# Starting a recurrent layer's first group beside the last projections and norms of the attention layer before it

## The chip, the cores and the metric

The kernel runs on one core of one Trainium2 chip. The metric is the device time of one execution in microseconds (us), as the median of several runs. All matrix work is in float32.

## What is computed

Four layers follow one another on a hidden state of 16 sequences x 100 tokens x 512 channels: a grouped-query cross-attention (layer 0, 32 query heads, 8 key heads, 361 context tokens), a recurrent block of the RWKV kind (layer 1), a cross-attention with an MLP (layer 2), and a second recurrent block (layer 3). The two that the change touches, cut down:

```python
# layer 0, end: attention output, residual, norm
out = out @ Wo + bo
x = out + hidden_state
mu, var = x.mean(-1), x.var(-1)
x = (x - mu) * rsqrt(var + 1e-6) * gamma + beta

# layer 1, start (the "front")
xa = _ln(x, ln1_w, ln1_b)
sx = concatenate([state[:, 1:2] - xa[:, :1], xa[:, :-1] - xa[:, 1:]], axis=1)
xxx = tanh((xa + sx * maa_x) @ maa_w1).reshape(b, l, 5, DM)
xxx = einsum('blfd,fde->blfe', xxx, maa_w2)
xk, xw, xv, xr, xg = xa + sx * (maa_stack + xxx)      # five mixes
w = exp(-exp(time_decay + tanh(xw @ td_w1) @ td_w2))
r, k, v = xr @ Wr.T, xk @ Wk.T, xv @ Wv.T             # then a scan over the tokens
```

## The kernel before

The hidden state X stays in on-chip memory, channels on the partitions: 4 channel chunks (C = 4) of 128, and 1600 tokens along the free axis. There are 8 groups of 200 tokens (N = 200, two sequences each), and 4 pairs of groups. Each engine has its own instruction stream, in order; the streams meet only in semaphores. A signal's value at(i, n) counts n events of turn i, and an engine waits for it with wait_ge.

**The end of layer 0** works on pairs. For a pair t TensorE does two projections of one group each (project, line 314, 16 matmuls, which the trace counts as 32 records) into banks 4, 5 and 6, 7. DVE adds bias and residual in 8 instructions (line 1468). The norm of a pair (class Norm) takes, for each group: four accumulated matmuls for the mean (line 237), DVE's centring of 800 elements (line 243), ACT's square (247), four accumulated matmuls for the variance (252), on ACT a logarithm (258) and an exponential (261), each with a load of its table, DVE's scaling (266), and four affine activations on ACT into X (1547). The matmuls for pair t+1's projection stand behind the variances of pair t in TensorE's stream (behind_it), DVE's residual of pair t+1 behind its scaling of pair t. The loop has 3 turns, and a fourth norm without a projection stands behind it. All of layer 0 is over with the signal norm_ready.at(pairs), which layer 1 knows as after.done.

**The front of layer 1.** Function rwkv builds body(i, g, front, rec, back, tail) for every engine; a turn holds the front of group g+1, the recurrence of group g (rec), the output and the second norm of group g-1 (back) and the end of the MLP part of group g-2 (tail). turns() calls it first with the front of group 0 alone. Before that every engine waits for after.done, and for its weights. In the front: mean (bank 7), centring, square, variance, logarithm, exponential, scaling, affine into xs (963), the token shift on DVE (800, 804), the hidden projection on TensorE (600, 602), tanh on ACT (1010, 1011), and then five mixes, each four small matmuls (523), four DVE instructions (mix_term, 731) and an addition on POOL (1087), followed by projections (509). K's first half is evicted by ACT (1024), V's first half too (925). V goes through SP's queue to memory and comes back spread over the partitions (448, 465); with it, and with a start column from ACT (914), DVE can begin the recurrence: product (708) and scan (723). SP's stream waits for "columns", three small DVE memsets.

Layer 1's weights lie over buffers of layer 0 that are free once attention is over, so SP loads all of them from then on (L_w in the trace).

**Layer 2** already has the class FoldedNorm: DVE adds the four channel chunks in two instructions (lines 281 and 283 for the mean, 292 and 294 for the variance), and TensorE then needs one matmul where Norm has four (287, 298); its logarithms and exponentials are separate calls (302, 307), so two groups can share a table load. Its query loop (projection 314, evictions 1927) is in the trace of before as well.

Of the kernel before, what the change touches and what calls it, by code (L numbers as in the profile page):

```python
# [15 lines left out]
C = D // P  # L16
# [134 lines left out]
class Layer:  # L151
# [3 lines left out]

    def __init__(self, sync, tensor, vector, scalar, gpsimd, done, early, left, pieces):
        self.sync, self.tensor, self.vector, self.scalar, self.gpsimd = sync, tensor, vector, scalar, gpsimd
        self.done, self.early, self.left, self.pieces = done, early, left, pieces

# [232 lines left out]
def rwkv(core, m, name, base, after):  # L392
# [78 lines left out]
    occ = base // G  # L471

    def turns(eng, body):
# [12 lines left out]


    def tensor(pe):
        def body(i, g, front, rec, back, tail):
# [55 lines left out]
            if front:  # L545
                m.n1.pe_var(pe, f)
            if back:
                reduce(7, b)
# [46 lines left out]
            if front:  # L595
# [90 lines left out]
    def vector(dve):  # L686
        def body(i, g, front, rec, back, tail):
# [61 lines left out]
            if front:  # L749
# [3 lines left out]
                if back:  # L753
                    wait(dve, "bonus_sum", b, 1)
                m.n1.dve_center(dve, xg(g + 1), f)

            step(1)
# [18 lines left out]
            if front:  # L776
                m.n1.scale(dve, f)

            step(3)
# [15 lines left out]
            if front:  # L795
# [7 lines left out]
                for c in range(C):  # L803
                    dve.scalar_tensor_tensor(seq(m.xx)[:, c], seq(m.sx)[:, c], vec("maa_x", c), m.xs[:, c, :, 1:E],
                                             ALU.mult, ALU.add).then_inc(sem("xa_shifted"), 1)

            step(6)
# [21 lines left out]
            if front:  # L829
                if rec:  # L830
                    wait(dve, "k_sum", i, 2)
                mix_term(0)
            if back:
                wait(dve, "out_sum", b, 2)
# [8 lines left out]
            if front:  # L843
                if rec:
                    wait(dve, "decay", i, 4)
                mix_term(1)

            step(10)
# [12 lines left out]
            if front:  # L861
                if rec:
                    wait(dve, "r_sum", i, 2)
                mix_term(3)

# [25 lines left out]

        core.wait_before(dve, after)
        wait(dve, "weights", occ + 1)

        dve.memset(m.we.rearrange("p c j (b e) -> p (c j b) e", b=NB)[:, :, 0:1], 0.0).then_inc(sem("columns"), 1)
        dve.memset(m.k.rearrange("p c b e -> p (c b) e")[:, :, 0:1], 1.0).then_inc(sem("columns"), 1)
        dve.memset(m.v.rearrange("p c b e -> p (c b) e")[:, :, 0:1], 0.0).then_inc(sem("columns"), 1)
        turns(dve, body)


    def scalar(act):
        def body(i, g, front, rec, back, tail):
# [44 lines left out]
            if front:  # L947
                if tail:
                    act.wait_ge(m.n2.nrm.sem, m.n2.nrm.at(t, 1))
                m.n1.act_rstd(act, f)  # L950
            if back:
                if tail:
# [5 lines left out]
            if front:  # L958
# [3 lines left out]
                for c in range(C):  # L962
                    act.activation(m.xs[:, c, :, 1:E], seq(m.n1.yc)[:, c], ACT.Identity, bias=vec("ln1_b", c),
                                   scale=vec("ln1_w", c)).then_inc(sem("xa"), 1)
            if back:
                wait(act, "head_var", b, 1)
# [39 lines left out]
            if front:  # L1006
                wait(act, "mix_hidden_sum", f, 1)
                if rec:
                    wait(act, "mix_sum", i, 5)
                act.activation(m.tha, chunk(7, 0), ACT.Tanh).then_inc(sem("mix_hidden"), 1)  # L1010
                act.activation(m.thl[BACK:BACK + DM, :], chunk(7, 1, BACK, BACK + DM), ACT.Tanh).then_inc(
                    sem("mix_hidden"), 1)

            start(10)
# [102 lines left out]
def gqa_attention(core, name, after):  # L1117
# [101 lines left out]
    def tensor(pe):  # L1219
# [126 lines left out]

        def output(t):

            for u in range(2):
                pe.wait_ge(residual_added.sem, residual_added.at(t))  # L1350
                src = lambda k: qT[:, k, bass.ds(t * (2 * N) + u * N, N)]
                project(pe, core, 2 + u, Wo, src).then_inc(out_sum.sem, 1)

        def behind_it(t, more):

            for u in range(2):
                pe.wait_ge(residual_added.sem, residual_added.at(t, 4 * u + 4))
                norms[u].pe_mean(pe, lambda c: X[:, c, bass.ds(t * (2 * N) + u * N, N)], t)
            for u in range(2):
                norms[u].pe_var(pe, t)  # L1360
            if more:
                for u in range(2):
                    pe.wait_ge(residual_added.sem, residual_added.at(t, 4 * u + 4))
                    project(pe, core, 2 + u, Wo,
                            lambda k: qT[:, k, bass.ds(t * (2 * N) + 2 * N + u * N, N)]).then_inc(out_sum.sem, 1)

        output(0)
        with pe.Fori(0, pairs - 1) as t:
            behind_it(t, True)
        behind_it(pairs - 1, False)  # L1370


    def vector(dve):
# [84 lines left out]

        def xo(t, u):
            return X[:, :, bass.ds(t * (2 * N) + u * N, N)]  # L1460

        def residual(t):

            for u in range(2):
                dve.wait_ge(out_sum.sem, out_sum.at(t, u + 1))
                x = xo(t, u)
                for c in range(C):
                    dve.scalar_tensor_tensor(x[:, c, :], part(2 + u, c), vec_("bo", c), x[:, c, :], ALU.add,
                                             ALU.add).then_inc(residual_added.sem, 1)

        def behind_it(t, more):
            for u in range(2):
                dve.wait_ge(residual_added.sem, residual_added.at(t, 4 * u + 4))
                dve.wait_ge(norm_ready.sem, norm_ready.at(t))
                norms[u].dve_center(dve, xo(t, u), t)
            for u in range(2):
                norms[u].scale(dve, t)
            if more:
                residual(t + 1)

        residual(0)
        with dve.Fori(0, pairs - 1) as t:
            behind_it(t, True)
        behind_it(pairs - 1, False)


    def scalar(act):
# [50 lines left out]
        turns(act, step)  # L1538
        with act.Fori(0, pairs) as t:
            for u in range(2):  # L1540
                norms[u].act_square(act, t)
            for u in range(2):
                norms[u].act_rstd(act, t)
            for u in range(2):
                norms[u].wait_scaled(act, t)
                for c in range(C):
                    act.activation(X[:, c, bass.ds(t * (2 * N) + u * N, N)], norms[u].yc[:, c, :], ACT.Identity,
                                   bias=vec_("beta", c), scale=vec_("gamma", c)).then_inc(norm_ready.sem, 1)


    def gpsimd(pool):
# [31 lines left out]
        for u in range(2):  # L1583
# [3 lines left out]
                 (attention_ready.sem, attention_ready.at(TURNS)), left,  # L1587
                 (pairs, lambda t: (norm_ready.sem, norm_ready.at(t, 8))))

# [733 lines left out]
```

## Time and profile before

| | us |
|---|---|
| median of 3 runs (3078.34 to 3083.32) | 3081.06 |
| the profiled execution's own time | 3076.93 |
| its span in the profile | 3075.0 |
| TensorE busy (share of the span) | 2811.2 (91%) |
| DVE busy | 2003.5 (65%) |
| ACT busy | 1350.9 (44%) |
| POOL busy | 665.0 (22%) |
| mean granted TensorE clock (1 is 2.4 GHz) | 0.962 |

The profile is of one execution. All stretches further down are in us from the start of its span. A busy engine is not an engine at its peak: matmuls are pipelined, and their ends are modelled.

### The profile page before, as it was taken

Reading aid. Unit: us, or ns where it says so; the run is one execution under the profiler, and the core shown is the slowest. Engines: PE = TensorE matmul, PEld = TensorE weight load, DVE = VectorE, ACT = ScalarE, POOL = GpSimd, SP = SyncE. Lnnn points to the kernel's source line nnn. Section 1 sums busy time; section 2 is a strip of 40 time slices with the busy share of each in tenths; the row PEclk is TensorE's granted clock in tenths of the full one; section 3 lists DMA queues with packets and bytes.
Section 4 is the critical chain, followed back from the end, with each engine's and each line's share of the span. In section 5 each row is a group of like instructions: output and inputs, shape, how many; then the busy total and the mean of one; then the engine's idle time right before and its main releaser. Section 6 shows DMA issues by size and latency. Waiting matters only on the chain.

```text
span 3075.0 us, 53764 instructions
## 1 busy us (share of the span) xinstructions
PE 2811.2 (91%) x18112; PEld 2186.9 (71%) x18112; DVE 2003.5 (65%) x4888; ACT 1350.9 (44%) x3446; POOL 665.0 (22%) x436
## 2 busy tenths in 40 slices
PE   7999999967999999779999999999997889999986
PEld 7555555856888888666555455799996768888866
DVE  2878787338999999644555556511101699999993
ACT  1888888542443443343444444332311234444432
POOL 0111110015444444300000000000000454444440
PEclk9999999978999999889999999999998899999998
DMA  2100100313333333300000000300002333333340
GB/s 107 36 24 34 34 23 13 130 41 98 92 92 90 88 91 92 107 27 10 30 20 19 26 22 10 126 26 1 0 1 89 92 95 92 89 92 92 87 126 14
DMA packets 96167, 182.85 MB, mean 59 GB/s; under 512 B 10122, under 2 KB 87498, under 8 KB 92462
## 3 DMA queue, kind: packets, MB, share of 16 engines
q1 hardware_dynamic: 96046, 181.27, 19.2%
q8 instruction: 72, 1.18, 0.2%
q14 instruction: 49, 0.40, 0.0%
HBM read 171.34 MB, written 9.90 MB: 59 GB/s over the span
## 4 chain that ended last, share of the span: by engine, by line
PE 66%; DVE 12%; issue 9%; ACT 8%; DMA 2%; POOL 1%; SPq 0%; DVEq 0%; ACTq 0%; POOLq 0%
PE psum L509 19%; PE psum L314 10%; PE psum L1859 6%; PE psum L1746 4%; PE psum L1303 3%; DVE psum L708 3%; PE psum L500 3%; ACT arena L1506 3%; ACT arena L2126 2%; PE psum L1759 2%; PE psum L1801 2%; PE psum L516 2%; PE psum L1315 2%; DVE arena L723 2%; PE psum L523 2%
## 5 line engine op out<-in xcount | busy, mean ns | idle before, releaser
L509 PE MATMUL psum<-arena 128*128 128x200 f32 x4096 | 772.1, 347 | 51.5 <-DVE arena L876 18.6
L509 PEld LDWEIGHTS psum<-arena 128*128 128x128 f32 x4096 | 721.9, 198 | 135.6 <-issue 79.3
L1107 POOL TENSOR_TENSOR arena<-arena 128x800 f32<-128x800 f32 x256 | 454.9, 1780 | 452.2 <-DVE psum L708 452.2
L723 DVE TENSOR_TENSOR_SCAN arena<-arena,psum 128x808 f32<-128x808 f32 x256 | 470.0, 1836 | 37.3 <-PE psum L500 22.1
L314 PE MATMUL psum<-arena 128*128 128x200 f32 (+1 forms) x1920 | 332.1, 335 | 15.0 <-POOLq L139 13.3
L314 PEld LDWEIGHTS psum<-arena 128*128 128x128 f32 x1920 | 328.5, 192 | 16.7 <-POOLq L139 13.3
L1506 ACT ACTIVATE arena<-arena 100x361 f32<-100x361 f32 x512 | 300.6, 590 | 87.2 <-DVE arena L1417 85.5
L1087 POOL TENSOR_TENSOR arena<-arena 128x800 f32<-128x800 f32 x80 | 140.6, 1757 | 807.6 <-DVE arena L731 632.3
L708 DVE TENSOR_TENSOR psum<-arena 128x808 f32<-128x808 f32 x256 | 280.6, 1096 | 5.5
L1417 DVE CUSTOM_DVE_ANT_0 arena<-psum,arena 100x361 f32<-100x361 f32 x512 | 254.3, 531 | 45.4 <-ACT arena L1506 37.9
L1303 PEld LDWEIGHTS psum<-arena 100*128 100x128 f32 x1536 | 146.3, 142 | 131.2 <-ACT arena L1518 60.3
L2126 ACT ACTIVATE arena<-arena 100x361 f32<-100x361 f32 x256 | 149.6, 587 | 146.5 <-DVE arena L1999 146.5
L1303 PE MATMUL psum<-arena 100*128 100x100 f32 x1536 | 189.5, 258 | 24.3 <-ACT arena L1518 24.1
L1801 PEld LDWEIGHTS psum<-arena 100*128 100x128 f32 x768 | 84.5, 141 | 148.8 <-issue 74.8
L1759 PE MATMUL psum<-arena 128*128 128x512 f32 (+1 forms) x384 | 189.4, 605 | 0.0
L1746 PE MATMUL psum<-arena 128*128 128x361 f32 x512 | 180.2, 477 | 1.6 <-DVE arena L1927 1.5
L1859 PE MATMUL psum<-arena 128*128 128x200 f32 x1024 | 175.0, 333 | 0.1
L1859 PEld LDWEIGHTS psum<-arena 128*128 128x128 f32 x1024 | 173.4, 190 | 0.4 <-DMA arena<-L_fc 0.4
L914 ACT ACTIVATE arena<-arena 128x8 f32 (+1 forms) x256 | 54.1, 212 | 267.7 <-DMA arena<-v_rows 266.7
L247 ACT ACTIVATE arena<-arena 128x800 f32<-128x800 f32 x56 | 48.7, 870 | 262.3 <-DVE arena L243 262.1
L731 DVE SCALAR_TENSOR_TENSOR arena<-psum,arena 128x200 f32<-128x200 f32 x320 | 112.9, 415 | 57.8 <-PE psum L523 57.8
L500 PE MATMUL psum<-arena 128*32 128x400 f32 x1024 | 127.6, 537 | 23.8 <-POOL arena L1107 14.2
(142 smaller groups left out, 3908.3 us busy)
## 6 DMA issues: line engine op xcount, KB each, us to landing
arena<-v_rows SPq DMA_DIRECT2D x512, 202.0 KB, 3.2
arena<-ctxT SPq DMA_DIRECT2D x32, 722.0 KB, 4.2
arena<-L_w SPq DMA_DIRECT2D x9, 1024.0 KB, 10.5
arena<-L_w SPq DMA_DIRECT2D x8, 1152.0 KB, 16.1
v_rows<-arena SPq DMA_DIRECT2D x32, 202.0 KB, 2.1
arena<-L_fc SPq DMA_DIRECT2D x4, 1024.0 KB, 8.3
arena<-L_pj SPq DMA_DIRECT2D x4, 1024.0 KB, 15.5
arena<-xT SPq DMA_DIRECT2D x4, 800.0 KB, 12.0
```

The costliest lines, as they stand in the source:

```text
L314: mm = pe.matmul(core.part(w, m), weight[:, k, m * P:(m + 1) * P], src(k), start=k == 0, stop=k == k_chunks - 1)
L500: mm = pe.matmul(psum[r0:r0 + 32, 6, 0:2 * N], core.red_w[:, 24 - 8 * q:56 - 8 * q], rv[:, h, :, 0:L], start=q == 0, stop=q == 3)
L509: mm = pe.matmul(chunk(bank, j), m.W[n][:, k, c * P:(c + 1) * P], src[:, k, :], start=k == 0, stop=k == C - 1)
L708: dve.tensor_tensor(m.kv.rearrange("p (h x) -> p h x", h=2), kb, m.spread[n % 4].rearrange("p h a e -> p h (a e)"), ALU.mult).then_inc(sem ...
L723: dve.tensor_tensor_scan(m.ring[n % 4].rearrange("p j e -> p (j e)"), m.we[:, cc].rearrange("p j e -> p (j e)"), m.kv, 0.0, ALU.mult, ALU. ...
L1107: pool.tensor_tensor(sv, sv, rb, ALU.mult).then_inc(sem("r_states"), 1)
L1303: mm = pe.transpose(bank[4 + 3 * (n % 2)][:, j * L:(j + 1) * L], pr[h % 8][0:L, j * P:(j + 1) * P], ident[0:L, 0:L])
L1417: dve.tensor_tensor_reduce(out=sm[n][0:L], in0=bank[n][0:L, 0:S], in1=nmask[u][0:L], scale=1.0, scalar=FLT, op0=ALU.add, op1=ALU.min, accu ...
L1506: act.activation(pr[k % 8][0:L, 0:S], sm[n][0:L], ACT.Exp, bias=nmx[0:L, k:k + 1], scale=-1.0, accum_out=den[0:L, k:k + 1]).then_inc(exp_r ...
L1746: mm = pe.matmul(bank[6 + c % 2][:, 0:S], Wk[:, k, c * P:(c + 1) * P], ctxt[u % 2][:, k, :], start=k == 0, stop=k == C - 1)
L1759: mm = pe.matmul(bank[6 + j % 2][0:n, :], ctxt[u % 2][:, k, a:a + n], Wv[:, k, :], start=k == 0, stop=k == C - 1)
L1859: mm = pe.matmul(part(2 + q % 2, m), fc[:, k, j * P:(j + 1) * P], norms[u].yc[:, k, :], start=k == 0, stop=k == C - 1)
```

## The change

There are three parts.

- Layer 0's norms become FoldedNorm, with one table load for the logarithms and one for the exponentials of a pair.
- The loop at the end of layer 0 has two turns in place of three, in another order: TensorE does the first projection of pair t+1, the means of pair t, the second projection of pair t+1, the variances of pair t.
- What is left of layer 0 (the projections of pair 3, the norms of pairs 2 and 3) is handed to layer 1 as after.tail, three functions for TensorE, DVE and ACT. The first body() of rwkv, with the front of group 0 alone, calls them through rest() at fixed places. It starts when pair 0 is normalized (after.pieces[1](0)) instead of when layer 0 is over; the wait for after.done comes behind it, on DVE ahead of the fourth mix term, where the memsets of the columns now stand.

```diff
     def turns(eng, body):
-        core.wait_before(eng, after)
+        if after.tail:
+            eng.wait_ge(*after.pieces[1](0))
+        else:
+            core.wait_before(eng, after)
         wait(eng, "weights", occ + 1)
         body(base - 1, -1, front=True, rec=False, back=False, tail=False)
+        if after.tail:
+            core.wait_before(eng, after)
...
                 m.n1.pe_mean(pe, lambda c: X[:, c, ds(g + 1, N)], f)
+                rest(0, pe, "out 6", front, rec)
...
                 m.n1.pe_var(pe, f)
+                if not rec and after.tail:
+                    rest(0, pe, "means 2", front, rec)
+                    pe.wait_ge(m.n1.lnv.sem, m.n1.lnv.at(f, 1))
+                    rest(0, pe, "out 7", front, rec)
...
                 mm.then_inc(sem("mix_hidden_sum"), 1)
+                rest(0, pe, "means 3", front, rec)
...
                 mix(0)
+                rest(0, pe, "variances 3", front, rec)
...
                 wait(pe, "mixed", f, 2)
+                rest(0, pe, "bank 3 read", front, rec)
...
-    norms = [Norm(core, told, u, 1, 2 * u, 2 * u + 1).memory(r) for u in range(2)]
+    folds = s("folds", 8)
+    norms = [FoldedNorm(core, told, u, 1, 2 * u, 2 * u + 1).memory(r).signals(folds) for u in range(2)]
...
+        for u in range(2):
+            pe_output(pe, 0, u, True)
+        with pe.Fori(0, pairs - 2) as t:
+            pe_output(pe, t + 1, 0, False)
+            pe_means(pe, t)
+            pe_output(pe, t + 1, 1, False)
+            pe_variances(pe, t)
+        pe.wait_ge(residual_added.sem, residual_added.at(pairs - 2, 8))
...
+    p, z = pairs - 2, pairs - 1
+    def pe_tail(pe, k):
+        if k == "out 6":
+            pe_output(pe, z, 0, False)
+        if k == "means 2":
+            pe_means(pe, p)
+        if k == "out 7":
+            pe_output(pe, z, 1, False)
+            pe_variances(pe, p)
+            pe.wait_ge(residual_added.sem, residual_added.at(z, 8))
+        if k == "means 3":
+            pe_means(pe, z)
+        if k == "variances 3":
+            pe_variances(pe, z)
+        if k == "bank 3 read":
+            pe.wait_ge(norms[1].lnv.sem, norms[1].lnv.at(z, 2))
+    def dve_tail(dve, k):
+        if k == "centre 2":
+            dve_fold(dve, p)
+            dve_residual(dve, z, 0)
+            dve_centre(dve, p)
+        if k == "squares 2":
+            dve_squares(dve, p)
+        if k == "centre 3":
+            dve_residual(dve, z, 1)
+            dve_scale(dve, p)
+            dve_fold(dve, z)
+            dve_centre(dve, z)
+        if k == "squares 3":
+            dve_squares(dve, z)
+        if k == "scale 3":
+            dve_scale(dve, z)
+    def act_tail(act, k):
+        if k == "squares 2":
+            act_squares(act, p)
+        if k == "rstd 2":
+            act_rstd(act, p)
+        if k == "norm 3":
+            act_affine(act, p)
+            act_squares(act, z)
+            act_rstd(act, z)
+            act_affine(act, z)
+    def dve_centre(dve, t):
+        for u in range(2):
+            dve.wait_ge(norm_ready.sem, norm_ready.at(t))
+            norms[u].dve_center(dve, xo(t, u), t)
+        with dve.Fori(0, pairs - 2) as t:
+            dve_fold(dve, t)
+            dve_residual(dve, t + 1, 0)
+            dve_centre(dve, t)
+            dve_squares(dve, t)
+            dve_residual(dve, t + 1, 1)
+            dve_scale(dve, t)
+        with act.Fori(0, pairs - 2) as t:
+            act_squares(act, t)
+            act_rstd(act, t)
+            act_affine(act, t)
```

On DVE the pieces stand behind the front's centring (centre 2), its scaling (squares 2), the token shift (centre 3), mix term 0 (squares 3) and mix term 1 (scale 3); on ACT behind the front's exponential (squares 2), the affine into xs (rstd 2) and the tanh of the hidden projection (norm 3). The new dve_centre waits for norm_ready.at(t), that is, for all affines of the pairs before t, as behind_it did.

## Rows read from the trace of the kernel before

**Rows 1.** Busy time by stage: us, busy us of each engine, granted clock, DMA share, GB/s.
```profile
551.80:632.10 80.30, 68.42 (x384) 64.43 (x384) 26.76 (x48) 48.10 (x72) 0.00 (x0) 0.97 0.31 124
632.10:678.60 46.50, 33.86 (x144) 28.25 (x144) 11.72 (x32) 11.09 (x23) 6.93 (x4) 0.75 0.08 23
```
**Rows 2.** Chain that ended last, pieces in order of time: start, us, what.
```profile
582.41 1.63 PE psum L237 x8
584.18 1.00 DVE arena L243
585.20 0.88 ACT arena L247
586.12 1.62 PE psum L252 x8
587.74 10.84 PE psum L314 x64
...
600.28 1.63 PE psum L237 x8
```
**Rows 3.** Timeline, first projections of layer 0's end: start, us, engine, line, work, idle before.
```profile
551.85 11.10 PE L314 MATMUL psum<-arena 128*128 128x200 f32 x64 [0.70 <-DVE arena L1451]
...
562.98 1.43 DVE L1468 SCALAR_TENSOR_TENSOR arena<-psum,arena 128x200 f32<-128x200 f32 x4 [3.99 <-PE psum L314]
```
**Rows 4.** Timeline, one turn of layer 2's query loop, with folded norms.
```profile
1371.19 0.57 DVE L281 TENSOR_TENSOR arena<-arena 128x400 f32 x1
1371.79 0.37 DVE L283 TENSOR_TENSOR arena<-arena 128x200 f32<-128x200 f32 x1
...
1373.54 5.58 PE L314 MATMUL psum<-arena 128*128 128x200 f32 x32
...
1378.96 0.84 PE L298 MATMUL psum<-arena 128*128 128x200 f32 x4
...
1381.98 1.89 DVE L266 TENSOR_TENSOR arena<-arena 128x800 f32<-128x800 f32 x2 [1.26 <-ACT arena L307]
...
1383.79 0.57 DVE L281 TENSOR_TENSOR arena<-arena 128x400 f32 x1
```
**Rows 5.** Timeline, the norm of layer 0's last pair.
```profile
616.27 1.52 PE L237 MATMUL psum<-arena 128*128 128x200 f32 x8
...
621.73 1.28 ACT L258 ACT_TABLE_LOAD   x1
...
623.02 0.43 ACT L258 ACTIVATE arena<-psum,arena 128x200 f32<-128x200 f32 x1
...
628.46 3.65 ACT L1547 ACTIVATE arena<-arena 128x200 f32 x8
```
**Rows 6.** Busy time in one turn of layer 0's last loop.
```profile
581.00:599.00 18.00, 17.17 (x99) 16.25 (x98) 6.79 (x13) 12.03 (x18) 0.00 (x0) 1.00 0.00 0
```
**Rows 7.** Timeline, layer 1's front of group 0.
```profile
637.26 3.04 PE L252 MATMUL psum<-arena 128*128 128x200 f32 x8 [2.06 <-ACT arena L247]
...
648.01 3.03 PE L600 MATMUL psum<-arena 128*128 128x200 f32 x8 [7.71 <-DVE arena L804]
...
650.97 1.93 PE L602 MATMUL psum<-arena 128*32 128x200 f32 x8
...
658.72 4.59 PE L509 MATMUL psum<-arena 128*128 128x200 f32 x16 [0.28 <-POOL arena L1087]
...
671.20 0.50 ACT L925 ACTIVATE arena<-psum 128x400 f32<-128x400 f32 x1 [4.48 <-PE psum L509]
...
678.54 1.00 DVE L708 TENSOR_TENSOR psum<-arena 128x808 f32<-128x808 f32 x1
```
**Rows 8.** Busy time and granted clock (third last column) in slices of 1 us.
```profile
623.00:624.00 1.00, 0.38 (x3) 0.07 (x1) 0.00 (x0) 0.97 (x3) 0.00 (x0) 1.00 0.00 0
...
628.00:629.00 1.00, 0.00 (x0) 0.00 (x0) 0.41 (x1) 0.99 (x4) 0.00 (x0) 0.50 0.00 0
...
651.00:652.00 1.00, 1.00 (x5) 0.61 (x5) 0.00 (x0) 0.00 (x0) 0.00 (x0) 0.60 0.00 0
```

More of the change, by code:

```diff
@@ L471, in rwkv, with rest @@
     occ = base // G
+    def rest(n, eng, k, front, rec):
+        if front and not rec and after.tail:
+            after.tail[n](eng, k)
     def turns(eng, body):
-        core.wait_before(eng, after)
+        if after.tail:
+            eng.wait_ge(*after.pieces[1](0))
+        else:
+            core.wait_before(eng, after)
         wait(eng, "weights", occ + 1)
         body(base - 1, -1, front=True, rec=False, back=False, tail=False)
+        if after.tail:
+            core.wait_before(eng, after)
         wait(eng, "weights_back", occ + 1)
@@ L755, in body @@
                 m.n1.dve_center(dve, xg(g + 1), f)
+                rest(1, dve, "centre 2", front, rec)
             step(1)
@@ L777, in body @@
                 m.n1.scale(dve, f)
+                rest(1, dve, "squares 2", front, rec)
             step(3)
@@ L805, in body @@
                                              ALU.mult, ALU.add).then_inc(sem("xa_shifted"), 1)
+                rest(1, dve, "centre 3", front, rec)
             step(6)
@@ L832, in body @@
                 mix_term(0)
+                rest(1, dve, "squares 3", front, rec)
             if back:
@@ L846, in body @@
                 mix_term(1)
+                rest(1, dve, "scale 3", front, rec)
             step(10)
@@ L863, in body @@
                     wait(dve, "r_sum", i, 2)
+                if not rec and after.tail:
+                    dve.wait_ge(*after.done)
+                    columns()
                 mix_term(3)
@@ L890, in body, with columns @@
             step(15)
[L892 to L897, printed above, removed]
+        def columns():
+            dve.memset(m.we.rearrange("p c j (b e) -> p (c j b) e", b=NB)[:, :, 0:1], 0.0).then_inc(sem("columns"), 1)
+            dve.memset(m.k.rearrange("p c b e -> p (c b) e")[:, :, 0:1], 1.0).then_inc(sem("columns"), 1)
+            dve.memset(m.v.rearrange("p c b e -> p (c b) e")[:, :, 0:1], 0.0).then_inc(sem("columns"), 1)
+        if not after.tail:
+            core.wait_before(dve, after)
+            wait(dve, "weights", occ + 1)
+            columns()
         turns(dve, body)
@@ L950, in body @@
                 m.n1.act_rstd(act, f)
+                rest(2, act, "squares 2", front, rec)
             if back:
@@ L964, in body @@
                                    scale=vec("ln1_w", c)).then_inc(sem("xa"), 1)
+                rest(2, act, "rstd 2", front, rec)
             if back:
@@ L1012, in body @@
                     sem("mix_hidden"), 1)
+                rest(2, act, "norm 3", front, rec)
             start(10)
@@ L1344, in tensor @@
         pe.wait_ge(attention_ready.sem, attention_ready.at(TURNS))
[L1347 to L1370, printed above, removed]
+        for u in range(2):
[6 more added lines that the diff above has]
+        pe.wait_ge(residual_added.sem, residual_added.at(pairs - 2, 8))
+    def pe_output(pe, t, u, first):
+        if not first:
+            pe.wait_ge(residual_added.sem, residual_added.at(t, 4 * u - 4))
+        src = lambda k: qT[:, k, bass.ds(t * (2 * N) + u * N, N)]
+        project(pe, core, 2 + u, Wo, src).then_inc(out_sum.sem, 1)
@@ new lines, in pe_means, with pe_variances, xo, dve_residual @@
+    def pe_means(pe, t):
+        for u in range(2):
+            norms[u].pe_mean(pe, t)
+    def pe_variances(pe, t):
+        for u in range(2):
+            norms[u].pe_var(pe, t)
+    def xo(t, u):
+        return X[:, :, bass.ds(t * (2 * N) + u * N, N)]
+    def dve_residual(dve, t, u):
+        dve.wait_ge(out_sum.sem, out_sum.at(t, u + 1))
+        x = xo(t, u)
+        for c in range(C):
+            dve.scalar_tensor_tensor(x[:, c, :], part(2 + u, c), vec_("bo", c), x[:, c, :], ALU.add,
+                                     ALU.add).then_inc(residual_added.sem, 1)
@@ new lines, in act_squares, with act_rstd, act_affine @@
+    def act_squares(act, t):
+        for u in range(2):
+            norms[u].act_square(act, t)
+    def act_rstd(act, t):
+        for u in range(2):
+            norms[u].act_log(act, t)
+        for u in range(2):
+            norms[u].act_exp(act, t)
+    def act_affine(act, t):
+        for u in range(2):
+            norms[u].wait_scaled(act, t)
+            for c in range(C):
+                act.activation(X[:, c, bass.ds(t * (2 * N) + u * N, N)], norms[u].yc[:, c, :], ACT.Identity,
+                               bias=vec_("beta", c), scale=vec_("gamma", c)).then_inc(norm_ready.sem, 1)
@@ L1457, in vector @@
         turns(dve, step)
[L1459 to L1484, printed above, removed]
+        for u in range(2):
+            dve_residual(dve, 0, u)
+        with dve.Fori(0, pairs - 2) as t:
[5 more added lines that the diff above has]
+            dve_scale(dve, t)
     def scalar(act):
```

27 lines of the change are left out of this document (14 added, 13 removed).

## The prediction

> **What bounds the kernel now.** I read the page, then the busy time by stage, then the chain that ended last, then the timeline of the stretch that the change touches. TensorE is busy 91% of the span, but not evenly. The stage in question runs from the last attention turn of layer 0 to the first recurrence step of layer 1. It has two parts [rows 1]: 80.3 us of output projections and norms, with 68.4 us of TensorE work at nearly full clock, and 46.5 us of layer 1's front for its first group, with 33.9 us of TensorE work at a mean granted clock of 0.75. In the first part the chain goes through TensorE's mean sums, DVE's centring, ACT's square, TensorE's variance sums, and then 10.84 us of projection for the next pair; a turn lasts 600.28 - 582.41 = 17.87 us [rows 2]. The projections start at 551.85 and the first pair's end at 562.95 [rows 3]. In the second part nothing overlaps: one group's 200 tokens go through every engine in turn.
>
> **The change part by part.** I lay out the new order engine by engine with the durations that rows show. Every step is on the path unless I say what covers it.
>
> *A, first projections.* Unchanged, 551.85 to 562.95, 11.1 us [rows 3].
>
> *B, the loop, now two turns instead of three and a last one.* The folded norm swaps the four accumulated matmuls of a mean or variance for two DVE additions (0.57 and 0.37 us) and one matmul. Layer 2's query loop already has this very mix: 64 projection records, four folded means and four folded variances (two records each), on DVE two folds, two centrings, two square folds, two scalings and 8 evictions, on ACT the same two table loads. Its turn is 1383.79 - 1371.19 = 12.60 us [rows 4]. The order differs: here a pair's scaling precedes its successor's fold, and the fold precedes a residual. Scaling ends about 4.9 us after the variances start (there from 1378.96 to 1381.98 + 1.89 [rows 4]), both folds by 6.7 us, against 0.7 + 5.6 us of variances and projection on TensorE, so the next mean waits some 0.3 us at most; I take 12.6 us and keep 13.2 us for the bound. DVE has about 10.3 us a turn and ACT 9.4, so neither is the bound. Two turns: 562.95 to 588.15. The additions cost nothing because TensorE's 11 us of projections lie over them; without that cover the eight would cost 4 x (0.57 + 0.37) = 3.8 us a turn.
>
> *C, up to layer 1's first hidden projection.* TensorE waits for the second residual of pair 2: projection end 587.3, 1.43 us of residual [rows 3], 588.8. Then the front's mean at the full clock 1.6 us (as in the chain [rows 2]), half of the last projection 5.5, the front's variance 1.6: 597.5. ACT's affine of pair 1 begins some 4 us after the last variances, about 591.4, takes 3.65 us [rows 5], and the front's square ends 0.9 later, just as TensorE gets there. Before, the variance ended at 637.26 + 3.04 = 640.30 and the hidden projection began at 648.01, 7.7 us later [rows 7]. That repeats, plus 0.65 us as ACT first squares pair 2, plus 1.45 us, because TensorE then waits for the last residual and DVE does it behind the token shift: 607.3. The other half projection (5.5 us, from about 598.4) and pair 2's sums are covered by those 7.7 us.
>
> *D, hidden projection to V's first eviction.* Before: 648.01 to 671.70, 23.7 us [rows 7]. Changes: hidden projections at full clock take 3.2 us, not 4.9, so -1.7. ACT, behind the tanh, now does pair 2's eight affines (3.65 us [rows 5]); DVE's centring of pair 3 waits for all of these, lasts 1.9 us, and the first mix term is queued behind it: mix term 0 starts about 4.0 us late. Then DVE's square folds, and TensorE's variances ahead of the second mix: +2.5. TensorE has by then stood idle for about 6.5 us. Before, the clock was at full at 623 as the last variances ended, at 0.50 (1.2 GHz) by 628 with nothing in between, and back only in the slice at 651, with work since 648 [rows 8]; so I let that mix run slow: +0.9. K's half projection, partly slow before (4.59 us [rows 7]), takes 3.0: -1.6. Pair 3's scaling and its affine lie beside K's projection and the next mixes; K's eviction on ACT slides behind the affine but is wanted only for V's projection, and the wait for the layer's end before the columns are cleared is over about 629.6. Sum 23.7 - 1.7 + 4.0 + 2.5 + 0.9 - 1.6, less 0.3 for the shorter wait at mix 3: 27.5 us, so V is evicted at 634.8.
>
> *E, eviction to the first product.* 671.70 to 678.54, 6.8 us [rows 7], a store, its reload and the in-order fifth mix term; no piece of it is touched: 641.6.
>
> *What is moved past queues.* SP gets nothing new. The weights of layer 1 were issued at the end of attention and the DMA is quiet from 581 on [rows 6], while the front wants them at 588. POOL's first addition follows mix term 0 as ever. ACT's table loads fall by two a pair (one logarithm and one exponential load serve both halves), which is worth 2.6 us of ACT a turn off the path. In the rows a load lasts 1.28 us and the next activation starts at 623.02, 1.29 us after the load began [rows 5]. The Trainium skill (ScalarE: Activation LUTs, What ACT_TABLE_LOAD costs) puts every switch at about 2.66 us, a drain included; by that some three loads on the new path would add 4.1 us and the estimate would be 3048. The trace shows no such drain.
>
> **The sum.** 11.1 + 25.2 + 19.2 + 27.5 + 6.8 = 89.8 us in place of 126.7, so 36.9 us less. The profiled execution took 3076.93 us around a span of 3075.0 and lies 4.1 us under the median of the runs. So I expect a span near 3038, and 3081.06 - 36.9 = 3044.2 us for the median. The rest of the kernel only slides. Bounds: handoffs between engines, which I put at what rows show (about 0.05 us), occur some 40 times on the new path; at 0.2 us each, +6. Full clock throughout, -1.5 to -3. If the loop's turn is 13.2, +1.2. If the centring of pair 3 did not hold mix term 0, -4. The recurrence after it meets another clock phase: some 5 us either way.
>
> **The rivals.**
> 1. *The merged stage does not merge:* the front waits for something that comes late, and only the loop gains. Three turns at 12.6, then the unmerged last norm (616.3 to 632.1, 16 us [rows 5]) and the front (46.4 us) put the first product at 562.95 + 37.8 + 16 + 46.4 = 663.1, a gain of 15.4: 3065.7. For it: three queues share one order, and each wait sits in front of two layers' work. Against it: the gates, pair 0's norm (about 582.5) and the weights (581), pass before the queues get there.
> 2. *The wait in D is longer:* ACT carries affine, squares, logarithms and affine again before it evicts K. If every step came a handoff late or ACT's queue held V's projection, D would be 8 to 14 us longer, V starting after the affine instead of beside it: 3052 to 3058.
> 3. *The other sign, the clock:* TensorE has about 38 us of full-speed work between 588 and 641. If its clock sat at 0.50 for all of it, from the small folded sums and the waits between them, these 38 us would double and take back the whole 36.9: 3082, slower by a hair. It decides only if practically all of that work runs slow. Speaking for it: the old front had 0.75 in the mean [rows 1]. Against it: the clock stays at full over the loop, whose gaps are under 1 us, and fell in an idle stretch of four us and more [rows 8]; I find one such stretch in the new order.
> 4. *More than forecast:* no clock loss, no held mix term: 37 + 4 + 3, 3037.
>
> **How the numbers follow.** Forecast with its bounds (3038 to 3051) 0.74; rival 2 0.11; rival 4 0.06; rival 1 0.05; rival 3 or the like, 0.04. The range 3036 to 3057 leaves out rivals 1 and 3 and the ends of 2 and 4, some 15 in 100. Within 0.2% is 6.2 us, about what a measurement of this kernel can tell from no change (the three runs shown span 5 us). Faster by more takes rivals 1, 2, 4 and the forecast: 0.95; same 0.02; slower 0.03.
>
> **What would show it.** Right: a loop turn near 12.6 us with TensorE idle under 1 us in it; the front's mean at about 589; hidden projection at about 607; DVE's centring of pair 3 released by ACT's affine, and mix term 0 right behind it at 617; clock 0.50 for some microseconds around 618 to 624; the first product at about 642, and the distance from there to the end unchanged at 2396 us. Wrong: a turn of 14 us or more with DVE released late, the first product past 650, or a changed distance from the first product to the end.

## The result and the profile after

| | before | after |
|---|---|---|
| median (range), us | 3082.19 (3078.34 to 3084.07) | 3046.87 (3044.82 to 3053.31) |
| profiled execution, span | 3075.0 | 3046.6 |
| TensorE busy, mean granted clock | 2811.2, 0.962 | 2794.7, 0.961 |

The ratio is 0.9891, 95% interval 0.9872 to 0.9909: 35.3 us less between the medians, where 36.9 was forecast. The median before is now that of four runs, 1.1 us above the one shown ahead.

In the file after the change the lines have moved: the residual is line 1414, layer 0's affines 1449, the hidden projection 615 and 617, the mixes 533, the projections 519, DVE's mix terms 749, POOL's addition 1120, V's eviction 955, the product 726.

The first loop turn in the timeline after the change. These lines answer to [rows 2] and are those of layer 2's loop in [rows 4] over again:

```profile
569.00 5.58 PE L314 MATMUL psum<-arena 128*128 x32
...
574.41 0.84 PE L298 MATMUL psum<-arena 128*128 128x200 f32 x4
...
581.59 5.58 PE L314 MATMUL psum<-arena 128*128 x32
...
587.00 0.84 PE L298 MATMUL psum<-arena 128*128 128x200 f32 x4
```

From one pair of variances to the next it is 587.00 - 574.41 = 12.59 us, against 17.87 before and 12.60 forecast. Now the merged part, as the chain that ended last goes through it (start, us, what), against [rows 5, 7]:

```profile
606.65 2.12 PE psum L615 x8
608.77 2.62 PE psum L617 x8
...
611.42 0.34 ACT arena L1042
...
611.78 0.33 ACT arena L1043
...
612.13 3.67 ACT arena L1449 x8
...
615.83 0.04 DVE arena L243
...
616.74 0.98 DVE arena L243
617.72 1.34 DVE arena L749 x4
619.05 0.49 DVE arena L292
...
619.57 1.79 DVE arena L294
...
621.40 1.92 PE psum L298 x4
623.33 2.96 PE psum L533 x8
626.29 5.50 PE psum L519 x16
631.79 1.56 PE psum L533 x8
```

The lines show a queue from engine to engine: tanh, then pair 2's affines on ACT, then pair 3's centring and the mix term on DVE, then the square folds, pair 3's variances, the second mix, and K's projection. Three durations in it are new. A square fold of 200 elements takes 1.79 us, the second mix 2.96, and K's projection 5.50. The hidden projection started at 606.65 (forecast 607.3), V was evicted at 639.69 + 0.50 = 640.19, and the first product started at 647.03 (forecast 641.6).

A span alone would not be a good meter for what follows. Outside the stretch of the change all kernels below run the same instructions, and yet in their profiles layer 1 from its first product to layer 2's first fold took between 663.5 and 671.3 us, and the rest between 1728.5 and 1736.0. So each run is read by its stretch, from DVE's first residual (557.57 before, 557.69 after) to the first product (678.54, 647.03): 121.0 us before, 89.3 after, 31.6 less. The start of the scan behind the product is given too, since a product can start and then be held up. The timed medians stand beside them; between variants of the change they tell little.

### The profile page after: what moved, and what is told of

Its sections match the earlier page's. It is cut to its first block, busy times and chain, and to the rows that moved or that the text cites. A ratio compares the mean times of both kernels' runs of the same rounds, so it can differ in the third digit from the quotient of the medians.

```text
span 3046.6 us, 53530 instructions
## 1 busy us (share of the span) xinstructions
PE 2794.7 (92%) x18016; PEld 2172.7 (71%) x18016; DVE 2018.4 (66%) x4920; ACT 1340.0 (44%) x3438; POOL 665.8 (22%) x436
## 4 chain that ended last, share of the span: by engine, by line
PE 67%; DVE 13%; issue 10%; ACT 8%; POOL 1%; DMA 1%; DVEq 0%; SPq 0%; ACTq 0%; POOLq 0%
PE psum L519 20%; PE psum L314 10%; PE psum L1964 6%; PE psum L1851 4%; PE psum L1337 3%; DVE psum L726 3%; PE psum L510 3%; ACT arena L1617 3%; ACT arena L2231 2%; PE psum L1864 2%; PE psum L1906 2%; PE psum L526 2%; PE psum L1349 2%; DVE arena L741 2%; PE psum L533 2%
## 5 line engine op out<-in xcount | busy, mean ns | idle before, releaser
L314 PEld LDWEIGHTS psum<-arena 128*128 128x128 f32 x1920 | 328.4, 192 | 16.9 <-POOLq L139 13.3
L533 PE MATMUL psum<-arena 32*128 32x200 f32 x640 | 135.4, 352 | 12.1 <-DVE arena L749 5.8
```

What stands on the lines that cost most here:

```text
L314: mm = pe.matmul(core.part(w, m), weight[:, k, m * P:(m + 1) * P], src(k), start=k == 0, stop=k == k_chunks - 1)
```

## Experiments

| kernel | stretch, us | to hidden projection | from there | first residual to first scan | median | ratio to before, 95% interval |
|---|---|---|---|---|---|---|
| before | 121.0 | 90.4 | 30.5 | 122.0 | 3082.19 | |
| after | 89.3 | 49.0 | 40.4 | 90.4 | 3046.87 | 0.9891 (0.9872 to 0.9909) |
| again | 89.4 | 49.0 | 40.5 | 90.5 | 3046.29 | 0.9886 (0.9868 to 0.9903) |
| fold_only | 107.7 | 77.5 | 30.2 | 108.7 | 3069.31 | 0.9967 (0.9955 to 0.9979) |
| merge_only | 92.9 | 57.9 | 35.0 | 94.8 | 3058.16 | 0.9921 (0.9903 to 0.9939) |
| merge_again | 92.5 | 57.9 | 34.5 | 94.6 | 3051.18 | 0.9903 (0.9886 to 0.9919) |
| affine_early | 85.7 | 49.0 | 36.8 | 86.8 | 3046.59 | 0.9889 (0.9871 to 0.9907) |
| pool_late | 87.3 | 49.0 | 38.4 | 89.8 | 3046.56 | 0.9882 (0.9865 to 0.9898) |
| filler | 83.5 | 49.0 | 34.6 | 84.6 | 3046.49 | 0.9887 (0.9870 to 0.9903) |
| early_late | 84.3 | 49.0 | 35.3 | 85.3 | 3044.60 | 0.9875 (0.9860 to 0.9890) |
| early_late_filler | 84.7 | 49.0 | 35.8 | 85.7 | 3042.92 | 0.9870 (0.9853 to 0.9886) |
| combined2 | 79.6 | 49.0 | 30.6 | 80.6 | 3046.31 | 0.9885 (0.9870 to 0.9900) |
| pair3_unfolded | 84.6 | 49.0 | 35.7 | 85.7 | 3046.09 | 0.9882 (0.9866 to 0.9898) |
| pair3_unfolded_early | 80.9 | 49.0 | 32.0 | 82.0 | 3041.93 | 0.9863 (0.9847 to 0.9880) |

The stretches are differences of two starts in one profile each, rounded after the difference was taken. Each ratio is to the kernel before as timed in the same comparison (medians 3079.64 to 3084.04). Edits are against the changed kernel.

**Each half alone.** First folding without merging:

```diff
-        with pe.Fori(0, pairs - 2) as t:
+        with pe.Fori(0, pairs - 1) as t:
...
-        pe.wait_ge(residual_added.sem, residual_added.at(pairs - 2, 8))
+        pe_means(pe, pairs - 1)
+        pe_variances(pe, pairs - 1)
...
-                 (pairs, lambda t: (norm_ready.sem, norm_ready.at(t, 8))), (pe_tail, dve_tail, act_tail))
+                 (pairs, lambda t: (norm_ready.sem, norm_ready.at(t, 8))))
```

(DVE and ACT alike: all pairs are finished in layer 0, and layer 1 starts behind them.)

> Layer 0 gets the folded norms and the new order of its loop (three turns, then the last norm), and layer 1 starts behind it as before; nothing is merged. By the sum in the prediction a turn takes 12.6 us instead of 17.87 and the first product starts at 663 instead of 678.5, a gain of about 15 us (0.5%). If folding were free of effect because the loop was bound by its chain of engines and not by TensorE, a turn would stay near 17.9 and the gain near 0.

The stretch lost 13.3 us, 2.1 less than the sum said; the turns were 12.6 us as expected (DVE's scalings at 590.37 and 602.97). The sum had taken 16 us for the last norm, the length of the unfolded one. In the timeline TensorE ends the last projection's turn with pair 2's variances at 599.95 + 0.84 = 600.79, and then waits 5.0 us for pair 3's fold, which stands behind pair 2's scaling on DVE:

```profile
599.95 0.84 PE L298 MATMUL psum<-arena 128*128 128x200 f32 x4
...
602.97 1.89 DVE L266 TENSOR_TENSOR arena<-arena 128x800 f32<-128x800 f32 x2 [1.28 <-ACT arena L307]
...
605.80 1.92 PE L287 MATMUL psum<-arena 128*128 128x200 f32 x4 [5.01 <-DVE arena L283]
...
615.97 3.67 ACT L1450 ACTIVATE arena<-arena 128x200 f32 x8 [0.89 <-DVE arena L266]
```

The norm ends at 619.64, 18.9 us behind the variances. With nothing of layer 1 to do meanwhile, that wait is on the path.

Then merging without folding:

```diff
+class PlainNorm(FoldedNorm):
+    def dve_fold(self, dve, src, i):
+        pass
+    def dve_fold_squares(self, dve, i):
+        pass
+    def pe_mean(self, pe, src, i):
+        Norm.pe_mean(self, pe, src, i)
+    def pe_var(self, pe, i):
+        Norm.pe_var(self, pe, i)
...
-    norms = [FoldedNorm(core, told, u, 1, 2 * u, 2 * u + 1).memory(r).signals(folds) for u in range(2)]
+    norms = [PlainNorm(core, told, u, 1, 2 * u, 2 * u + 1).memory(r).signals(folds) for u in range(2)]
```

> The merged order of the change with unfolded norms (four matmuls for each mean and variance, no additions on DVE). If folding and merging add up, a loop turn is about 17.5 us, the first product comes about 10 us later than the 647.0 of the change, less 1 to 3 us for the additions that DVE no longer does at the end: 654 to 657, a gain of 22 to 25 us. If merging alone gave the whole gain (the projections being hidden either way), the product would stay near 647.

The stretch was 92.9 us, 28.1 less than before. A turn took 16.2 us, not 17.5; in the new order half of a projection lies beside the centring and the squares, where before TensorE had none. The halves do not add: 28.1 alone and 13.3 alone, but 31.6 together. Up to the hidden projection folding is worth 57.9 - 49.0 = 8.9 us even in the merged order; behind it, it costs 40.4 - 35.0 = 5.4. Since the medians lay 11 us apart and the stretches only 3.6, both were run again on one chip.

> The merged order with unfolded norms a second time, beside the change on one chip. Within the stretch 92.9 us against 89.3, so 3.6 us behind the change; its medians of the first comparison lay 11 us behind. If folding is worth only what the stretch shows, the two medians are 3 to 5 us apart; if it also costs or saves something later, about 11 us.

> The changed kernel once more, unaltered, to run on the same chip as the three beside it. From the first residual of layer 0's end to the first product 89.3 us again, and a median 33 to 37 us below the kernel before. What differs outside that stretch from one profile to the next is the scatter that the other comparisons have to be read with.

The stretches repeated (92.5 and 89.4), and the medians were 4.9 us apart, so most of the 11 us was scatter. To the scan the two kernels are 4.1 and 4.5 us apart, not 3.0 and 3.6: with unfolded norms the product lasts 2.1 and 1.9 us instead of 1.0, because POOL's fifth addition starts just ahead of it.

**The queue on ACT.** Pair 2's affines go ahead of the tanh:

```diff
+                rest(2, act, "affine 2", front, rec)
                 wait(act, "mix_hidden_sum", f, 1)
...
+        if k == "affine 2":
+            act_affine(act, p)
         if k == "norm 3":
-            act_affine(act, p)
             act_squares(act, z)
```

> The change, but ACT does pair 2's eight affines ahead of the tanh of the hidden projection, where it stood idle for 4.7 us, instead of behind it. Theory queue: the centring of pair 3 comes 3.7 us earlier and everything behind it too, first product at 643.3 against 647.0. Theory queue and clock: TensorE's idle stretch also shrinks from 7.6 to about 4 us, part of the slow clock goes, and the product comes at 639 to 642. Theory that the clock and DVE's contention with POOL alone set the time: no change, 646 to 647.

3.6 us less, the queue's share and no more: the affines ran from 607.74, beside the hidden projection, and pair 3's centring began at 612.23, but TensorE still stood idle for 3.8 us ahead of pair 3's variances, the second mix took 3.03 us again and K's projection 5.70. Of the two theories with the queue in them, the one without a clock gain held.

**The clock.** Matmuls that nobody reads fill TensorE's two idle stretches:

```diff
+    def pe_keep_busy(pe, b, n):
+        for _ in range(n):
+            pe.matmul(bank[b][:, 0:N], ident, X[:, 0, 0:N], start=True, stop=True)
...
             pe_variances(pe, p)
+            pe_keep_busy(pe, 0, 6)
             pe.wait_ge(residual_added.sem, residual_added.at(z, 8))
...
         if k == "variances 3":
+            pe_keep_busy(pe, 6, 21)
             pe_variances(pe, z)
```

> The change, with matmuls whose result nobody reads in TensorE's two idle stretches: 6 behind pair 2's variances and 21 ahead of pair 3's variances. Nothing else is different. Theory clock: the hidden projection takes 3.2 us instead of 4.8, the second mix 1.6 instead of 3.0 and K's projection 3.0 instead of 5.6, so the first product comes at 641 to 642 instead of 647. Theory queue or contention alone: the product stays at 647, or comes later by what the extra matmuls overrun (up to 2 us).

The hidden projection comes 3.4 us later in this profile than in that of the change, as does the first residual; from the residual the stretch is 83.5 us, 5.8 less. In the timeline of this kernel (the extra matmuls are L1456):

```profile
610.01 1.62 PE L615 MATMUL psum<-arena 128*128 128x200 f32 x8 [0.51 <-DVE arena L1414]
...
611.56 1.54 PE L617 MATMUL psum<-arena 128*32 128x200 f32 x8
...
615.67 7.37 PE L1456 MATMUL psum<-arena 128*128 128x200 f32 x42
...
621.30 1.79 DVE L294 TENSOR_TENSOR arena<-arena 128x200 f32<-128x200 f32 x1
...
624.57 1.62 PE L533 MATMUL psum<-arena 32*128 32x200 f32 x8
...
626.12 2.97 PE L519 MATMUL psum<-arena 128*128 128x200 f32 x16
```

Hidden projection 3.2 us, second mix 1.6, K's projection 3.0, all at full clock, with ACT's queue and DVE's long fold as they were. From the hidden projection to V's eviction it is 637.72 - 610.01 = 27.7 us; the prediction had 27.5. That the two meet so closely is in part luck: the run still holds the 1.4 us of DVE's long fold, which the prediction did not have, and its second mix ran at full clock, where the prediction had added 0.9.

**POOL beside DVE.** POOL's additions 0 and 1 wait for DVE's square folds and scaling of pair 3:

```diff
                 wait(pool, "mix_term", f, 4 * x + 4)
+                rest(3, pool, x, front, rec)
...
+    def pool_tail(pool, x):
+        if x == 0:
+            pool.wait_ge(folds.sem, folds.at(z, 8))
+        if x == 1:
+            pool.wait_ge(norms[1].nrm.sem, norms[1].nrm.at(z, 2))
```

> The change, but POOL's first addition waits until DVE has folded pair 3's squares, and its second until DVE has scaled pair 3, so that they no longer run beside these. Theory contention: the second square fold lasts 0.37 us again instead of 1.78 and the two scalings 1.9 instead of 3.4; TensorE's variances of pair 3 start 1.4 us earlier, and the first product comes 1.4 us earlier in the stretch (87.9 instead of 89.3); the scalings' 1.5 us lie off the path. Theory that it is TensorE's clock that sets the time there: the same 1.4 us at most, or nothing if the slow clock only starts its work earlier. If the long duration has nothing to do with POOL, it stays at 1.78.

First the change's own timeline, DVE's lines and then POOL's:

```profile
619.57 1.78 DVE L294 TENSOR_TENSOR arena<-arena 128x200 f32<-128x200 f32 x1
621.27 0.56 DVE L292 TENSOR_TENSOR arena<-arena 128x400 f32<-128x400 f32 x1
...
627.67 3.43 DVE L266 TENSOR_TENSOR arena<-arena 128x800 f32<-128x800 f32 x2
```

```profile
619.23 1.90 POOL L1120 TENSOR_TENSOR arena<-arena 128x800 f32<-128x800 f32 x1 [71.29 <-DVE arena L749]
627.83 2.41 POOL L1120 TENSOR_TENSOR arena<-arena 128x800 f32<-128x800 f32 x1 [6.70 <-DVE arena L749]
```

and then the timeline with the additions moved (POOL's line is 1121 there):

```profile
619.73 0.37 DVE L294 TENSOR_TENSOR arena<-arena 128x200 f32<-128x200 f32 x1
...
621.16 1.73 POOL L1121 TENSOR_TENSOR arena<-arena 128x800 f32<-128x800 f32 x1 [73.06 <-DVE arena L294]
...
624.97 4.62 PE L519 MATMUL psum<-arena 128*128 128x200 f32 x16
...
626.42 1.89 DVE L266 TENSOR_TENSOR arena<-arena 128x800 f32<-128x800 f32 x2
...
628.45 1.74 POOL L1121 TENSOR_TENSOR arena<-arena 128x800 f32<-128x800 f32 x1 [5.56 <-DVE arena L266]
```

The fold is back at 0.37 us, the scalings at 1.89, POOL's additions at 1.73 and 1.74. The stretch fell by 2.0 us: 1.4 in the fold as expected, and K's projection took 4.62 us instead of 5.57 because the clock was back earlier in it. So the long durations were DVE and POOL keeping each other out. But most of the gain is gone one instruction later. POOL's fifth addition now starts 0.20 us ahead of the first product and holds it up:

```profile
644.98 1.73 POOL L1121 TENSOR_TENSOR arena<-arena 128x800 f32<-128x800 f32 x1 [7.44 <-DVE arena L749]
645.18 2.40 DVE L726 TENSOR_TENSOR psum<-arena 128x808 f32<-128x808 f32 x1 [0.28 <-ACT arena L944]
```

In the change the product started first (647.03, then POOL at 647.19) and took 0.99 us. To the scan this run is only 0.6 us faster, 89.8 us against 90.4.

**Together.** The two reorderings without extra matmuls (this expectation was written after the result of the run with extra matmuls, further down):

> Pair 2's affines early and POOL's first two additions late, without extra matmuls. The two shares found alone add up: 89.3 - 3.6 - 2.0 = 83.7 us. TensorE's idle stretch ahead of pair 3's variances shrinks to about 2.4 us. If the clock stays at full through so short a stretch, another 4 us go and it is 80; the hidden projection before it met a slow clock behind a stretch of 2.5 us, so I expect 83.7 rather.

84.3 us against 83.7: the two shares add up to within 0.6 us, though the clock took another course. The hidden projection ran at full clock here (1.62 and 1.54 us), behind the same 2.53 us of idleness as in the change; the clock fell at 613.8, in the first mix, and K's projection took 5.42 us. With extra matmuls (6 and 6) on top:

> Three edits on top of the change: pair 2's affines ahead of the tanh, POOL's first two additions behind DVE's square fold and scaling of pair 3, and unread matmuls in TensorE's gaps (6 and 6). If held queue, contention and slow clock are three separate shares, the stretch from the first residual to the first product falls from 89.3 to 89.3 - 3.6 - 1.4 - 5.7 = 78.6 us, and the median comes about 10 us below the change's, near 1.4% below the kernel before. If they are one and the same loss (the clock, which the shorter wait already mends), it stays at 82 to 84 us.

The forecast failed: 84.7, not 78.6. The first part went as meant (hidden 1.62 + 1.54, second mix 1.61, K 2.97), but the second edit to POOL made TensorE wait ahead of the decay projection, and further on the timeline reads:

```profile
624.49 2.22 PE L665 MATMUL psum<-arena 128*64 128x200 f32 x8 [0.75 <-POOL arena L1122]
...
626.65 3.03 PE L533 MATMUL psum<-arena 32*128 32x200 f32 x8
...
629.61 5.70 PE L519 MATMUL psum<-arena 128*128 128x200 f32 x16
```

The slow clock had only moved on, from K's projection to V's. So the same kernel without the wait ahead of POOL's second addition:

> As the run with three edits (84.7 us), but POOL's second addition is no longer held back, since there the wait opened gaps ahead of the decay projection, the clock fell at 625 and V's projection took 5.7 us. With the addition at once, TensorE's gaps are about 0.3 us each and V's projection takes 3.0 at full clock: the stretch is 80 us, and the median 9 us below the change's. If the clock falls again all the same, it stays at 84 to 85.

79.6 us, as expected, with V's projection at 2.97 us. Here the long scaling (3.43 us) is back and costs nothing. The median of its four timed runs (3046.31) does not show the gain: they scatter from 3039.8 to 3047.7.

**Folding only where it pays.** Pair 3's norm unfolded, the others folded:

```diff
         if k == "means 3":
-            pe_means(pe, z)
+            for u in range(2):
+                Norm.pe_mean(norms[u], pe, lambda c: xo(z, u)[:, c], z)
         if k == "variances 3":
-            pe_variances(pe, z)
+            for u in range(2):
+                Norm.pe_var(norms[u], pe, z)
...
             dve_scale(dve, p)
-            dve_fold(dve, z)
             dve_centre(dve, z)
-        if k == "squares 3":
-            dve_squares(dve, z)
```

> The change, but pair 3's norm, the last one, is unfolded: four matmuls for each mean and variance on TensorE, which stands idle there, and no additions on DVE, which has a queue. Theory that TensorE's idle stretch and the slow clock behind it are the loss: TensorE works until about 616.7 instead of 613.8, the second mix starts near 620 instead of 623 and runs at full clock, K's projection takes 3.0 us; the stretch from the first residual to the first product falls from 89.3 to about 84. Theory that folding is the better trade here too: TensorE's 4.6 us more of matmuls lengthen the stretch to 91 or more.

> The same with pair 2's affines ahead of the tanh. Here TensorE's unfolded means come before the first mix, so the centring of pair 3 is released at 613 to 615 instead of 615.8: about 1 us less than in the run beside it, a stretch of 83 to 83.5. If the held centring is a full share of its own (3.6 us as when it was moved alone), it is 80.

84.6 and 80.9 us. In the first the second mix takes 1.61 us and K's projection 2.97; in the second, where pair 3's variances too run at full clock, the timeline of TensorE is nearly without a hole:

```profile
611.74 3.03 PE L237 MATMUL psum<-arena 128*128 128x200 f32 x16
...
614.70 1.62 PE L533 MATMUL psum<-arena 32*128 32x200 f32 x8
...
616.24 2.97 PE L252 MATMUL psum<-arena 128*128 128x200 f32 x16
...
619.15 1.62 PE L533 MATMUL psum<-arena 32*128 32x200 f32 x8
...
620.69 2.98 PE L519 MATMUL psum<-arena 128*128 128x200 f32 x16
```

The held centring was a full share again (3.7 us), not the 1 us that I gave it: unmoved, the variances started 1.9 us after the first mix had ended and ran partly slow, 4.66 us. This version does only work that is needed, has a stretch 8.4 us shorter than the change, and the lowest ratio of all. Its interval (0.9847 to 0.9880) still overlaps that of the change (0.9868 to 0.9903 when run again), so by timed runs alone it is not shown to beat it.

## Why the prediction was right, and where its terms were off

By the medians the forecast of the whole, 36.9 us, met 35.3, and the direction and range held. In the stretch itself 31.6 us came; the miss lies in one term, D. By its own steps:

- *A and B:* right. First residual at 557.7 as before, turns of 12.59 us. TensorE did wait for the mean's fold, some 0.4 us in the second turn (1.25 us for what otherwise takes 0.84).
- *C:* right in place and size. The front's mean began at 588.79, the hidden projection at 606.65, 0.65 us ahead of the forecast, and the wait for the last residual stood directly before it.
- *D:* the mechanism was as put, with mix term 0 at 617.64 behind the held centring, but the term was mis-sized: 606.65 to 640.19 is 33.5 us, not 27.5. The miss is made of three pieces. The hidden projection was taken at full clock (3.2 us) and took 4.7, since the clock fell at 607.8 after a mere 2.5 us of idleness (in the profile of early_late it did not). Term 0 to the second mix was 5.6 us instead of 3.9, of which 1.4 is the fold that POOL held up; the prediction had put nothing for a POOL addition beside a fold. K's projection took 5.57 us instead of 3.0, since the clock stayed low until 631.5; the prediction had it low from 618 to 624, and it was low from 614.5 on. Together 1.5 + 1.7 + 2.6 = 5.8 of 6.0 us. The extra matmuls brought 5.8 us back, the moved additions 2.0 at the product and 0.6 at the scan; the shares overlap, as a shorter wait also shortens the slow clock.
- *E:* right, 640.19 to 647.03 is 6.8 us.
- *Table loads:* a load still took 1.28 us in the new order, with the logarithm 1.30 us behind its start (602.71 and 604.01). The Trainium skill (ScalarE: Activation LUTs, What ACT_TABLE_LOAD costs) gives about 1.38 us of drain for each such switch; the traces do not agree, here as before.
- *The sum:* the stretch gained 31.6 us where 36.9 was forecast, the profiled span 28.4, and the medians 35.3 and, run again, 37.8. From the first product to the end, which was to stay at 2396 us, it is 2399.6 (2397.6 in the second profile of the change, and 2397.7 to 2405.7 in the other variants). The profile of before is of an execution 5.3 us below the median of its kernel, that of the change 1.5 above, so before and after are further apart in their medians than in their profiles. The 5 us that D lost should show in the medians and do not. Whether something later in the kernel gives them back on average or the medians merely scatter stays open, and that the sum met the medians this closely is luck.
- *Rivals:* the merged stage did merge, and the layer's gates were passed early. D was longer, by 6.0 us where the second rival had 8 to 14, but through TensorE's clock and POOL, not through ACT: K's eviction came at 632.93, well ahead of V's projection at 636.68. The rival with the slow clock over all of the work did not come about: from 588 to 641 full clock alternated with two slow spells, of 3.2 and 17 us. What the prediction held against it was misread, though. It had the clock fall only in an idle stretch of four us and more, while the trace of before has a second fall behind gaps of 0.78 and 1.52 us (lines in the last section).

## What to carry to other kernels

Work that is pushed into another stage's idle time is paid for by what stands in the same queues: walk each engine's stream in order, and look for the instruction of the new work that the old chain now waits behind (here eight affines that could stand 4 us earlier). Taking matmuls away from TensorE helps where TensorE sets the pace and hurts where it waits; in the waiting stretch the unfolded norm was the cheaper one. Read such changes by the stretch that they touch, not by the span, when the rest of the kernel scatters by as much as the effect; and look one instruction past the mark at which the stretch ends, where a held instruction can take the gain back.

## What the runs showed of the hardware

TensorE's clock fell behind shorter idle stretches than the one that the prediction had read from [rows 8], and came back more slowly. Busy time and granted clock (third last column) of the changed kernel in slices of 1 us:

```profile
608.00:609.00 1.00, 1.00 (x4) 0.42 (x3) 0.97 (x3) 0.00 (x0) 0.00 (x0) 0.50 0.00 0
...
614.00:615.00 1.00, 0.00 (x0) 0.00 (x0) 0.00 (x0) 1.00 (x4) 0.00 (x0) 0.73 0.00 0
...
626.00:627.00 1.00, 1.00 (x3) 0.78 (x3) 0.67 (x2) 0.00 (x0) 0.00 (x0) 0.50 0.00 0
...
630.00:631.00 1.00, 1.00 (x4) 1.00 (x4) 1.00 (x1) 0.58 (x2) 0.24 (x1) 0.50 0.00 0
631.00:632.00 1.00, 1.00 (x5) 0.67 (x5) 0.10 (x1) 0.87 (x2) 0.00 (x0) 0.73 0.00 0
```

It was at 0.50 (1.2 GHz) in the slice from 608, though TensorE had been idle only from 604.1 to 606.65 and was working again; at 0.73 in the slice from 614, with the last mix ended at 613.8; and it was full (2.4 GHz) again only in the slice from 632, though TensorE had worked almost without a gap from 621.4 on. In [rows 8] the same fall had taken from 623.4 to 628, and the return less than 4 us of work. But the trace of before had a quick fall too, within K's first projection, behind gaps of 0.78 us (until 653.68) and 1.52 us (until 656.82):

```profile
658.00:659.00 1.00, 0.72 (x4) 0.41 (x3) 0.53 (x2) 0.00 (x0) 0.67 (x1) 0.81 0.00 0
...
662.00:663.00 1.00, 1.00 (x8) 1.00 (x6) 0.00 (x0) 0.00 (x0) 0.00 (x0) 0.98 0.00 0
```

And the same wait does not always end in the same clock. Seven profiles have TensorE idle for 2.5 us ahead of the hidden projection; in six the clock fell to 0.50 within it, and in early_late it stayed at 1.00:

```profile
609.00:610.00 1.00, 1.00 (x7) 0.58 (x6) 1.00 (x2) 1.00 (x3) 0.00 (x0) 1.00 0.00 0
...
613.00:614.00 1.00, 0.99 (x5) 0.99 (x6) 1.00 (x2) 0.56 (x1) 0.00 (x0) 0.92 0.00 0
```

So the price of an idle stretch cannot be read off its length; what else decides it, no run here shows.

DVE and POOL excluded each other for whole instructions where both inputs of DVE's instruction lay in SBUF (arena in these lines) and POOL read it too: a 0.37 us addition on DVE took 1.78 us, until the end of POOL's addition at 619.23 + 1.90 = 621.13; the second POOL addition, started 0.16 us into DVE's first scaling, took 2.41 us instead of 1.74, and the second scaling waited for it; and in pool_late the first product took 2.40 us instead of 1.00 behind POOL's fifth addition. The mix terms, which read one input from the matmul results, were never stretched: all 320 in the changed kernel took 0.40 to 0.43 us, some 100 of them while POOL was at work. The Trainium skill says this (SBUF — State Buffer, SBUF: two separate sides): the pair of ports that DVE and POOL share "is an exclusive lock, not a bandwidth split", which a DVE instruction with two SBUF inputs needs too. The traces agree, and moving the additions showed it.
